# A GRU over 256 steps: half 1's n transpose put behind half 0's scan of h on VectorE

## The reference

```python
    def _L0_cond_ref(x, w):                      # depthwise causal convolution, K taps per channel
        y = jax.lax.conv_general_dilated(x, w, window_strides=(1,), padding=[(K - 1, 0)], ...)
        return y
    ...
        def cell(h, x):
            gi = x @ W_ih + b_ih
            gh = h @ W_hh + b_hh
            i_r, i_z, i_n = jnp.split(gi, 3, axis=-1)
            h_r, h_z, h_n = jnp.split(gh, 3, axis=-1)
            r = jax.nn.sigmoid(i_r + h_r)
            z = jax.nn.sigmoid(i_z + h_z)
            n = jnp.tanh(i_n + r * h_n)
            h_new = (1.0 - z) * n + z * h
            return (h_new, h_new)
    ...
    x = x + _L0_cond_ref(x, cond_2048[:, None, :])
    x = x + _L1_cond_ref(cond_2048, x, L1_cond_W_ih, L1_cond_W_hh, L1_cond_b_ih, L1_cond_b_hh)
    return x
```

## Time and profile before

| | us |
|---|---|
| median of 3 runs | 988.08 (987.52 to 988.37) |
| the profiled execution | 988.25 |
| its span, first to last instruction | 986.4 |

### The profile page before, as it was taken

How to read it: one execution, slowest core, us unless ns; L and a number is a source line. 1 busy time by engine, 2 the same in 40 slices (tenths; PEclk the granted TensorE clock), 3 DMA queues, 4 the chain that set the end, 5 groups by cost and what they waited for, 6 DMA issues and landing times.

```text
span 986.4 us, 63804 instructions
## 1 busy us (share of the span) xinstructions
PE 974.2 (99%) x26660; PEld 793.8 (80%) x26660; DVE 881.4 (89%) x3075; ACT 514.1 (52%) x2158; POOL 558.3 (57%) x1589
## 2 busy tenths in 40 slices
PE   8999999999999999999999999999999999999997
PEld 5778888888888888888888888888888888888885
DVE  7879999999999999999999999999999988888565
ACT  5334455555555555555555555555555555555543
POOL 4556655556655555555555555655555555555542
PEclk9999999999999999999999999999999999999999
DMA  8731001010010101001010010100101000010000
GB/s 305 68 46 36 24 14 33 20 40 20 16 33 16 41 20 30 24 16 37 20 36 25 13 37 16 41 20 16 37 13 40 15 25 23 12 30 5 25 14 13
DMA packets 67024, 32.43 MB, mean 33 GB/s; under 512 B 44464, under 2 KB 65584, under 8 KB 66736
## 3 DMA queue, kind: packets, MB, share of 16 engines
q1 hardware_dynamic: 66304, 28.25, 11.2%
q10 hardware_dynamic: 432, 0.11, 0.0%
HBM read 19.86 MB, written 8.49 MB: 29 GB/s over the span
## 4 chain that ended last, share of the span: by engine, by line
PE 94%; SPq 3%; DMA 2%; DVE 0%; issue 0%; POOL 0%; ACT 0%; POOLq 0%; DVEq 0%
PE pg L807 66%; PE pcv L612 8%; PE pg L602 8%; PE pg L612 4%; PE pcv L622 4%; PE pcv L632 3%; DMA whh<-w_hh 2%; SPq L309 1%; SPq L303 1%; PE pg L592 1%; DMA xw<-x 0%; PE pcv L602 0%; SPq L334 0%; PE pcv L835 0%; DVE gt L1090 0%
## 5 line engine op out<-in xcount | busy, mean ns | idle before, releaser
L807 PE MATMUL pg<-whh,hp 128*32 128x192 f32 x16368 | 714.8, 327 | 5.0 <-DVE hp L1115 3.6
L807 PEld LDWEIGHTS pg<-whh,hp 128*32 128x32 f32 x16368 | 515.3, 110 | 133.4 <-DVE hp L1115 12.4
L1046 DVE SCALAR_TENSOR_TENSOR pcv<-xb,cnd,pcv 128x256 f32<-128x256 f32 (+2 forms) x588 | 315.0, 536 | 6.9
L998 ACT ACTIVATE rz<-gt 128x64 f32<-128x64 f32 x512 | 136.3, 266 | 293.7 <-DVE gt L1090 267.5
L569 POOL TENSOR_TENSOR nzh<-rz,hp 128x32 f32<-128x32 f32 x512 | 158.2, 309 | 210.7 <-ACT rz L998 209.0
L1090 DVE STREAM_TRANSPOSE gt<-pg 128x128 f32<-128x128 f32 x512 | 161.8, 316 | 50.2 <-PE pg L807 40.8
L1003 ACT ACTIVATE nzh<-an 128x32 f32<-128x32 f32 x512 | 120.9, 236 | 130.7 <-DVE an L1102 130.7
L1115 DVE TENSOR_TENSOR_SCAN hp<-zcp,nzh 128x96 f32<-128x96 f32 x512 | 173.5, 339 | 13.9 <-ACT nzh L1003 9.4
L1102 DVE TENSOR_TENSOR_SCAN an<-rz,gn 128x64 f32<-128x64 f32 x512 | 150.5, 294 | 26.7 <-ACT rz L998 26.7
L1000 ACT ACTIVATE zcp<-gt 128x32 f32<-128x32 f32 x512 | 111.0, 217 | 0.0
L1094 DVE STREAM_TRANSPOSE gn<-pg 128x64 f32<-128x64 f32 x512 | 106.9, 209 | 0.0
(11 more groups left out here) (116 smaller groups left out, 878.3 us busy)
## 6 DMA issues: line engine op xcount, KB each, us to landing
xb<-x SPq DMA_DIRECT2D x96, 94.0 KB, 2.0
out<-x SPq DMA_DIRECT2D x60, 128.0 KB, 1.8
wih<-w_ih SPq DMA_DIRECT2D x4, 768.0 KB, 8.1
whh<-w_hh SPq DMA_DIRECT2D x4, 768.0 KB, 14.6
xw<-x SPq DMA_DIRECT2D x24, 64.0 KB, 3.5
xb<-x SPq DMA_DIRECT2D x16, 62.0 KB, 1.9
tz<-taps SPq DMA_DIRECT2D x12, 64.0 KB, 3.6
xs<-x SPq DMA_DIRECT2D x1, 512.0 KB, 4.4
```

What stands on the lines that cost most here:

```text
L807: i = pe.matmul(pg[t // 2 % Q][f][D * j:D * (j + 1), 0:IN], hp[:, t % 2, 2 * c + 1 - t % 2:2 * c + 3 - t % 2, :, 1].rearrange("p u b -> p ...
L998: act.activation(rz[:, f, :, :, 1].rearrange("p g (c b) -> p (g c) b", b=B), gt[:, f, :, u], ACT.Sigmoid).then_inc(s_rz[f], 1)
L1046: dve.scalar_tensor_tensor(x1_of(c, a, b)[:, lo:hi] if lag == K - 1 else sums, xx[:, c, (K - 1 - lag) * B + lo:(K - 1 - lag) * B + hi], cn ...
```

## The change

On VectorE, transpose n of half 1 and scan h of half 0 change places, in all 256 steps. The columns that this transpose reads are those that TensorE overwrites next with `recur(t, 1, 0)`. Until now TensorE's wait for half 0 of h covered it, since scan h 0 stood behind the transpose; now it doesn't, and TensorE waits for `s_tn[1]` ahead of half 1's first matmul.

```diff
@@ TensorE, the loop over t @@
                 recur(t, 0, 1)
                 if t % 2 == 0:
                     pe.wait_ge(s_tin[1], m + 1)
+                pe.wait_ge(s_tn[1], t)
                 recur(t, 1, 0)
                 pe.wait_ge(s_h[1], t + 1)
                 recur(t, 0, 2)
@@ VectorE, the loop over t @@
                     transpose_in(i // H, i % H)
                 scan_n(t, 0)
                 transpose_rz(t, 1)
+                scan_h(t, 0)
                 transpose_n(t, 1)
-                scan_h(t, 0)
                 scan_n(t, 1)
                 for k, i in tapped(t):
                     long(k, i, LEFT)
```

## The result

| | before | after |
|---|---|---|
| median, us | 988.05 | 1024.04 (1023.84 to 1024.46) |
| profiled execution's span, us | 986.4 | 1022.1 |
| ratio | | 1.0368, 95% interval 1.0355 to 1.0381 |

The change makes the kernel 36.0 us slower. The direction was forecast; the size was 16.5, and the range ended at 1012.

A forecast was written before the change was run, and what follows sets the result against it. TensorE dominates the wait chain before (94%); afterwards a VectorE-ScalarE loop of 3.785 us binds full-tap steps. That adds 14.2 us, the remaining steps 2.3: +16.5 on 988.08 gives 1004.6 us, range 993.5 to 1012.

The forecast's parts named there:

- Part (3): VectorE and ScalarE, full-tap steps: a loop without TensorE closes at 3.785 us a step, +14.2 us over steps 12 to 203.
- Part (4): TensorE's new wait at half 1's first matmul: transpose ends at step start + 1.72, TensorE arrives at 2.29, covered by 0.57.
- Part (2): VectorE, half 1: scan n waits for the transpose directly ahead, starting 0.25 us after its start; scan n comes 0.17 later.
- The bound of 0.36: Upper bound from transpose start to scan n on VectorE: the longer r-z transpose of 0.32 plus 0.04.
- the main case: VectorE and ScalarE loop of 3.785 us in full-tap steps, 1004.6 us, 1000 to 1009; chance 70%.
- The first: Faster rival, VectorE: the transpose's wait costs only its slot, 0.13; loop 3.665, TensorE sets the pace, 985.0 us; chance 8%.
- Dearer: Rival, VectorE: scan h of half 0 doesn't move forward, stays at 1.31; loop 3.86, 1019.0 us; chance 14%.
- Only half 1 of h: Rival: loop of 3.70 to 3.74 swallowed by TensorE's long steps; only short steps pay, +5.7, 993.8 us; chance 8%.

## Why the prediction was right or wrong

**Right: the place, the loop and the cover.** Part (3) held: a loop closed through VectorE and ScalarE that leaves TensorE out, all full-tap steps became equally long, and the signs named for it came (steps of one length, scan h right behind its tanh, more waiting of TensorE for scan h, VectorE hardly waiting for TensorE). Two runs show it from both sides: 56 moved steps of 256 cost 2.9 us of the 36, and a filler in the wait makes the kernel slower by its own length less the wait. Part (4), the free wait of TensorE, held too.

**Wrong: the size, by one term.** Part (2) took 0.25 from the transpose's start to scan n; it is 0.32. The row it was read from, WHOLE behind RIGHT, is an instruction that carries the wait itself; scan n has its wait for the transpose in a separate instruction ahead of it, so that both the end of that one and the start of the scan come behind the transpose. The bound of 0.36 included it, but the main case's own range did not use that bound: "some 0.02 together". A term in a loop of 192 steps counts 192 times: the 0.055 of the separate wait is 10.6 us there, and late starts of half 1 are paid in other steps too. Of the 19.4 us between 1004.6 and 1024.0, the run with the semaphores in another order gave back 13.5.

What is left are the 6.0 us between its 1010.6 and my 1004.6. Some 5.5 are in the full taps (737.6 us there, 732.1 forecast): their steps are 3.805 and not 3.785, 0.02 x 192 = 3.8, in part because the transpose takes 0.23 there and not 0.21; the rest is in the steps that are longer for other reasons. The steps without taps lose 0.11 each and not 0.07. In that run's trace half 1 of h ends 0.17 later after the step's start than before (2.75 against 2.58), where I had 0.14; 0.09 was to spare, a little more than my 0.07; and by difference some 0.025 is TensorE's restart, which I had left out.

**The rivals.** The first is out: the dependent scan starts 0.32 behind the transpose, where an instruction that doesn't wait comes after 0.13. With it goes, for these instructions, what the Trainium skill ("VectorE: DVE Perf Modes", section "The DRAIN you can't avoid") found for eight tensor_copy, that a semaphore between VectorE instructions costs nothing extra. The same section says that an instruction that is not held starts earlier; I had left that out, and the 0.13 agrees with it. Another page of the Trainium skill ("Perfetto Trace Analysis") has a VectorE instruction wait in a queue of its own (section "DVE / Act Engine Instruction"), while one for the sequencer alone holds the sequencer up (section "Sequencer-only Instruction"); the 0.035 and the 0.09 of these runs fit that, though the page has no size for them. "Dearer" had the measured loop of 3.86 and a time near the result (1019), but by coincidence: its mechanism, scan h not moving forward, did not occur; it was at 1.23. "Only half 1 of h" exists as a second loop of 3.77, under the first.

**The expectation for the kernel before with the sigmoid's semaphore in the separate wait** failed on a point of the same kind: the late start was right, what it collided with was not looked at. GpSimd's product started at almost the same time in the record of before.

## What to carry to other kernels

Before an instruction is moved next to its consumer, look for what hid its latency; here it was the wait for the sigmoid, and 0.19 us of exposed latency closed a loop that ran 192 times. Then add up the loop that the new wait closes, term by term, and read each term from an instruction that waits in the same way: the last semaphore to arrive belongs on the instruction itself, not in the separate wait ahead of it. VectorE's busy share, 89% before and 88% after, said nothing of this.

## What the runs showed of the hardware

- On VectorE, an instruction that carries the wait starts 0.04 us after the end of the instruction it depends on; through a separate wait instruction it is 0.09. In the changed kernel the exchange of the two is 1024.0 against 1010.6 us.
- A scan of 128x64 with two inputs takes 0.29 us, and 0.40 when GpSimd's 128x32 product starts 0.01 ahead of it; its successor starts after 0.33 in place of 0.21. With the product 0.05 behind the scan's start it takes 0.29, and the product 0.31 in place of 0.27. With the product 0.11 ahead the scan takes 0.30, and with it 0.15 or more ahead 0.29 (the runs with the short WHOLE tap, with and without the scan's own wait).
- A matmul with one more semaphore to wait for, already satisfied, costs nothing measurable: 0.9996 of the time (0.9988 to 1.0005) with 255 such waits.
